# Attention over a running state: Q by the state of four sequences in one block of 32x32 tiles, and attention banks seeded with the result

## The chip, the cores and the metric

One core of one Trainium2 chip. The metric is the time of one execution on the device in microseconds (us); lower is better.

## What is computed

One transformer block on `x` of 4 sequences, 4096 tokens, 512 features, float32, 16 heads of 32 features: LayerNorm, causal linear attention, an output projection, LayerNorm and residual; then LayerNorm, a feed-forward layer with inputs and weights rounded to FP6 values with a scale per block of 32, LayerNorm and residual.

```python
q, k = elu(x @ Wq.T + bq) + 1, elu(x @ Wk.T + bk) + 1      # by heads
v = x @ Wv.T + bv
kv_cum = cumsum(einsum('bhtd,bhte->bhtde', k, v), axis=2)  # the state
numerator = einsum('bhtd,bhtde->bhte', q, kv_cum)
denominator = maximum(einsum('bhtd,bhtd->bht', q, cumsum(k, axis=2)), 1e-6)
out = (numerator / denominator) @ Wo.T + bo
x = x + layernorm(out)
x = x + layernorm(mx(layernorm(x)) @ mx(weight).T + bias)
```

## The kernel before, in words

The loop runs over 32 tiles of 128 tokens; a tile holds all four sequences, b = 0 to 3, 512 rows in all. `turn(i, ...)` is written once for each engine, and every engine carries out its steps in exactly that order; semaphores join them. A turn finishes the feed-forward of tile i-1, does the attention of tile i and begins the LayerNorm and transposes of tile i+1. The turns before and behind the loop leave out the part that does not exist.

Products against weights (k, q, v, o, f) are three products of rounded float32 halves (`product3`, L341): 12 matmuls of 512 columns. k(g) and q(g) write the four score banks, one for each group g of four heads. v, o, f, the transposes and the attention outputs share three PSUM banks, `work[0..2]`; `BANK_ORDER` (L36) lists which stage has which bank in which order, and `take` (L332) waits until the stage that had the bank before has been read (table `freed`, L236).

Attention of a sequence b: `scores(b)` (L426) is K by Q inside the tile, a product for each head, in the four score banks; `mask(b)` on VectorE (L868) applies the causal mask, four operations of 128x512, into A. `attend(b)` (L444) first multiplies Q by the state S, one 128x128 matmul for each group (S is kept block-diagonal, four heads of 32x32 in each group, zeros elsewhere, L453), then adds V by A for each head (L460). `state(b)` (L465) adds K by V of the tile to the state, which PSUM holds all the time; ScalarE copies it to S in four pieces for each sequence (L654). `o_hi` (ScalarE, L644) and `o_lo` (VectorE, L876) split the attention output in two halves, and `o(b)` multiplies it by Wo. Behind that stands a chain for each b: `o_bias` and statistics on VectorE, `rstd` on GpSimd (POOL), `o_norm` on ScalarE (L657), `residual` on POOL (L1049), `r_stats` on VectorE, `rstd`, `r_norm` on ScalarE (L660), `quantise` on VectorE (L893: amax, scale, reciprocal, and the product that writes q8), `dequantise` on POOL, transposes `xd` and f(b) in the next turn. Between them stand, for the next tile, `x_transposes(b)` on TensorE (PE), `x_hi(b)` and `x_norm(b+1)` on ScalarE and `x_lo(b)` on VectorE; x_norm(b+1) overwrites the tile xn that x_transposes(b) reads. Q is divided by the denominators (`denominators`, `invert`, `spread`, `divide`) before it is used.

The order on PE in the second half of a turn: kn(0), spread, f(3), scores(0), v(1), x(0), attend(0), state(0), kn(1), scores(1), v(2), o(0), x(1), attend(1), state(1), kn(2), scores(2), v(3), o(1), x(2), attend(2), state(2), kn(3), scores(3), x(3), o(2), attend(3), state(3); o(3) comes behind k(0) of the next turn. ScalarE's order there:

```python
kn(0); f_norm(2); x_hi(i + 1, 0); x_norm(i + 1, 1); o_hi(0); state(0); kn(1); f_norm(3)
x_hi(i + 1, 1); x_norm(i + 1, 2); o_hi(1); state(1); o_norm(i, 0); kn(2); r_norm(i, 0)
x_hi(i + 1, 2); x_norm(i + 1, 3); o_hi(2); state(2); kn(3); o_norm(i, 1); x_hi(i + 1, 3)
r_norm(i, 1); o_hi(3); state(3)
```

Of the kernel before, what the change touches and what calls it, by code (L numbers as in the profile page):

```python
# [12 lines left out]
P = 128  # L13
# [47 lines left out]
def build(nc, x, wq, wk, wv, wo, wf, bq, bk, bv, bo, bf, consts, out):  # L61
    ctx = ExitStack()
    with ctx:
# [47 lines left out]
        S = sb("S", [P, NSEQ, G, P])  # L111
# [78 lines left out]
        s_set = sem("s_set")  # L190
        xn_set = sem("xn_set")
# [36 lines left out]
        STAGE = {"k": V[:], "q": QT[:], "v": S[:].rearrange("p b g t -> p b (g t)"),  # L228
# [21 lines left out]
        def had_before(stage, here, before):  # L250
# [6 lines left out]
            return None  # L257

# [72 lines left out]
        def _(pe):  # L331
            def take(i, stage, here, before):  # L332

                found = had_before(stage, here, before)
                if found is None:
                    return
                other, turns = found
                reader, per = freed[other[0]]
                pe.wait_ge(reader, count(i + turns + tile_of(other), other[1], per))

# [17 lines left out]
            def transposes(stage, src):  # L358
                for g in range(G):
                    last = nc.tensor.transpose(bank(stage)[:, g * P:(g + 1) * P], src(g), ident[:])  # L360
                return last
# [14 lines left out]
            def turn(i, here, before):  # L376
# [16 lines left out]
                def v(b):  # L393
                    if cur:
                        take(i, ("v", b), here, before)
                        weights(i, "v")
                        by_row("v", b, xT_hi, xT_lo, slice(b * P, (b + 1) * P)).then_inc(v_mm, 1)

                def denominators():
                    if cur:  # L400
                        take(i, ("den", 0), here, before)
# [37 lines left out]
                def kn(b):  # L439
                    if cur:  # L440
                        take(i, ("kn", b), here, before)
                        transposes(("kn", b), lambda g: KT[:, g, b, SEG - P:SEG]).then_inc(kn_tr, 1)

                def attend(b):  # L444
                    if cur:
                        take(i, ("att", b), here, before)
                        if first:
                            pe.wait_ge(state_zeroed, 1)
                        else:
                            pe.wait_ge(s_set, count(i - 1, b))  # L450
# [731 lines left out]
```

## Time and profile before

| | us |
|---|---|
| median of 3 runs | 2689.52 (2688.79 to 2692.34) |
| the profiled execution | 2689.53 |
| its span, first to last instruction | 2687.7 |
| PE busy | 2503.3 (93%) |
| VectorE (DVE) busy | 2171.5 (81%) |
| ScalarE (ACT) busy | 1255.2 (47%) |
| GpSimd (POOL) busy | 1092.2 (41%) |

The share of busy time is an average over the run. What a step is worth is read from the timeline of one turn: an engine starts an instruction when the one before it on the same engine lets it and when what it waits for has been signalled. A timeline row gives the start and the duration; successive instructions of an engine overlap, so the step of an operation is the distance between two starts. The idle time in brackets names who ended it. A float32 matmul leaves two records, one in float32r one.

### The profile page before, as it was taken

The numbers are of one execution on the slowest core, as the hardware profiler recorded it, in microseconds if no ns is written. First come the engines' busy times: TensorE is split into PE (matmuls) and PEld (weight loads), VectorE is DVE, ScalarE is ACT, GpSimd is POOL, SyncE is SP. The second block draws the span as 40 slices with busy tenths as digits, with TensorE's granted clock in tenths as the row PEclk, the third lists the DMA queues.
The fourth block names the chain that finished last, engine by engine and source line by source line (L and its number), as shares of the span: only waits on it lengthen the run. The fifth ranks groups of instructions, "written<-read, shape, count | busy, mean of one in ns | idle before, by whom it ended". The sixth has DMA issues, their size and how long they took to land.

```text
span 2687.7 us, 62620 instructions
## 1 busy us (share of the span) xinstructions
PE 2503.3 (93%) x24082; PEld 2061.4 (77%) x24082; DVE 2171.5 (81%) x4175; ACT 1255.2 (47%) x2314; POOL 1092.2 (41%) x1482
## 2 busy tenths in 40 slices
PE   5999999999999999999999999999999999999996
PEld 4777778777778777778777787777777777877775
DVE  6778888788888788888888887888888888878885
ACT  4444445444454444454444544444544445444442
POOL 1343444334443334443344433444434444333443
PEclk8999999999999999999999999999999999999998
DMA  4011100111011111001111011110111110111000
GB/s 148 21 40 47 41 29 31 39 47 43 30 36 39 39 47 43 27 31 39 47 47 32 30 39 39 47 43 27 36 38 44 47 34 28 39 39 47 31 25 24
DMA packets 57483, 107.55 MB, mean 40 GB/s; under 512 B 6768, under 2 KB 7152, under 8 KB 56816
## 3 DMA queue, kind: packets, MB, share of 16 engines
q1 hardware_dynamic: 57456, 107.18, 12.3%
q8 instruction: 18, 0.29, 0.0%
q14 instruction: 9, 0.07, 0.0%
HBM read 73.60 MB, written 33.55 MB: 40 GB/s over the span
## 4 chain that ended last, share of the span: by engine, by line
PE 43%; DVE 29%; issue 11%; POOL 9%; ACT 6%; DVEq 1%; POOLq 0%; DMA 0%; ACTq 0%; SPq 0%
PE work L343 9%; PE work L345 8%; PE work L344 8%; DVE kc L829 6%; PE score L434 4%; DVE KT L812 4%; PE work L460 4%; PE work L360 4%; PE work L453 3%; DVE A L872 3%; POOL xd L1061 2%; DVE bn_r L789 2%; DVE amax L897 2%; POOL rs_r L1042 2%; DVE QT L812 2%
## 5 line engine op out<-in xcount | busy, mean ns | idle before, releaser
L872 DVE TENSOR_TENSOR A<-score,causal 128x512 f32<-128x512 f32 x512 | 317.5, 683 | 42.3 <-PE score L434 42.2
L597 ACT ACTIVATE o_buf<-x_res,shift_r,rs_r 128x512 f32<-128x512 f32 x128 | 104.7, 818 | 409.2 <-POOL shift_r L1045 409.2
L1052 POOL TENSOR_TENSOR x_res<-x_res,o_buf 128x512 f32<-128x512 f32 x128 | 179.3, 1401 | 210.4 <-ACT o_buf L597 210.4
L593 ACT CAST xT_hi<-work 128x512 fp32r<-128x512 f32 x128 | 74.8, 584 | 384.5 <-PE work L360 384.5
L343 PE MATMUL work<-wv_hi,xT_hi 128*128 128x512 f32 x512 | 216.1, 422 | 0.0
L343 PE MATMUL score<-xT_hi,wk_hi 128*128 128x512 f32 x512 | 206.6, 403 | 6.2 <-issue 6.2
L1042 POOL TENSOR_TENSOR rs_f<-ve_f,minus_half 128x1 f32<-128x1 f32 x128 | 70.3, 549 | 343.9 <-DVE ve_f L793 343.9
L1042 POOL TENSOR_TENSOR rs_r<-ve_r,minus_half 128x1 f32<-128x1 f32 x128 | 96.3, 753 | 278.5 <-DVE ve_r L793 278.5
L343 PE MATMUL score<-xT_hi,wq_hi 128*128 128x512 f32 x512 | 206.5, 403 | 0.0
L343 PE MATMUL work<-wo_hi,oT_hi 128*128 128x512 f32 x512 | 202.7, 396 | 2.9 <-DVE oT_lo L879 2.6
L344 PE MATMUL work<-wv_lo,xT_hi 128*128 128x512 f32 x512 | 202.0, 394 | 0.0
L345 PE MATMUL work<-wv_hi,xT_lo 128*128 128x512 f32 x512 | 201.4, 393 | 0.0
L345 PE MATMUL score<-xT_hi,wk_lo 128*128 128x512 f32 x512 | 200.4, 391 | 0.0
L344 PE MATMUL score<-xT_lo,wq_hi 128*128 128x512 f32 x512 | 200.3, 391 | 0.0
L344 PE MATMUL score<-xT_lo,wk_hi 128*128 128x512 f32 x512 | 200.2, 391 | 0.0
L345 PE MATMUL work<-wo_hi,oT_lo 128*128 128x512 f32 x512 | 200.1, 391 | 0.0
L345 PE MATMUL score<-xT_hi,wq_lo 128*128 128x512 f32 x512 | 199.9, 390 | 0.0
L344 PE MATMUL work<-wo_lo,oT_hi 128*128 128x512 f32 x512 | 199.3, 389 | 0.0
L1042 POOL TENSOR_TENSOR rs_o<-ve_o,minus_half 128x1 f32<-128x1 f32 x128 | 70.4, 550 | 303.9 <-DVE ve_o L793 303.7
L884 DVE TENSOR_TENSOR o_buf<-work,bias_o 128x512 f32<-128x512 f32 x128 | 87.9, 687 | 112.7 <-PE work L345 112.7
L453 PE MATMUL work<-QT,S 128*128 128x128 f32 x1024 | 138.4, 278 | 29.4 <-DVE xT_lo L803 29.4
L621 ACT ACTIVATE exp_t<-exp_t 128x512 f32<-128x512 f32 x256 | 161.1, 629 | 0.0
(130 smaller groups left out, 6957.9 us busy)
## 6 DMA issues: line engine op xcount, KB each, us to landing
x_in<-in_x SPq DMA_DIRECT2D x128, 256.0 KB, 2.8
x_res<-in_x SPq DMA_DIRECT2D x128, 256.0 KB, 2.6
out<-f_buf SPq DMA_DIRECT2D x96, 256.0 KB, 2.0
out<-xd SPq DMA_DIRECT2D x32, 256.0 KB, 2.0
V<-in_wk SPq DMA_DIRECT2D x1, 1024.0 KB, 7.8
QT<-in_wq SPq DMA_DIRECT2D x1, 1024.0 KB, 8.7
kc<-in_wo SPq DMA_DIRECT2D x1, 1024.0 KB, 10.2
A<-in_wf SPq DMA_DIRECT2D x1, 1024.0 KB, 11.9
```

Source lines behind the costliest of these rows:

```text
L343: nc.tensor.matmul(dst, st_hi(c), mv_hi(c), start=(c == 0), stop=False)
L344: nc.tensor.matmul(dst, st_hi(c), mv_lo(c), start=False, stop=False)
L345: last = nc.tensor.matmul(dst, st_lo(c), mv_hi(c), start=False, stop=(c == G - 1))
L360: last = nc.tensor.transpose(bank(stage)[:, g * P:(g + 1) * P], src(g), ident[:])
L434: last = nc.tensor.matmul(score_bank[j][:, g, :], KT[rows, g, b, SEG - P:SEG], QT[rows, g, cols], start=True, stop=True)
L453: nc.tensor.matmul(att[:, g, :], S[:, b, g, :], QT[:, g, b * P:(b + 1) * P], start=(g == 0), stop=False, skip_group_check=True)
L621: nc.scalar.activation(exp_t[:, g % 2, :], exp_t[:, g % 2, :], ACT.Exp, scale=-1.0).then_inc(exp_done, 1)
L812: nc.vector.tensor_tensor(dst, by_seq(exp_t[:, g % 2, :]), dst, ALU.add).then_inc(added, 1)
L829: nc.vector.tensor_tensor_scan(kc[:, g, :, :].rearrange("p b t -> p (b t)"), in_seq[:].rearrange("p b t -> p (b t)"), KT[:, g, :, :].rearr ...
L872: nc.vector.tensor_tensor(A[:, j, :, :], score_bank[j][:], causal[:].unsqueeze(1).to_broadcast([P, G, P]), ALU.mult).then_inc(a_set, 1)
L1042: nc.gpsimd.tensor_tensor(rs[n][:, b:b + 1], ve[n][:, b:b + 1], minus_half[:], ALU.pow).then_inc(rs_set[n], 1)
L1052: nc.gpsimd.tensor_tensor(x_res[:, b, :], x_res[:, b, :], o_buf[:, b % 2, :], ALU.add).then_inc(r_set, 1)
```

## The change

The products of Q with the state leave `attend(b)`. A new step `past_products` on PE, between f(3) and v(1), computes them for all four sequences, a 32x32 tile of the array for each head: rows j (head within the group), columns g (group), 64 matmuls of 128 columns into the four score banks. ScalarE copies the four banks to a new SBUF tile `past_att` (`past`), scores(0) wait for these copies, and before each attend(b) ScalarE copies that sequence's part into the attention bank (`seed`); V by A is added to it. v(1), v(2) and v(3) each stand one stage earlier on PE, mask(0) comes behind v_bias(1) and f_stats(3) on VectorE. S holds only the 32x32 blocks and is copied once a turn. The rows of the attention output change place, with Wo laid out to match on the host. `BANK_ORDER` changes with the order. The transposes set the start flag on the first of four only.

```diff
-    (("v", 1), W1), (("x", 0), W2), (("att", 0), W0), (("kn", 1), W2),
-    (("v", 2), W1), (("o", 0), W2), (("x", 1), W0), (("att", 1), W1), (("kn", 2), W0),
-    (("v", 3), W2), (("o", 1), W0), (("x", 2), W1), (("att", 2), W2), (("kn", 3), W1),
-    (("x", 3), W0), (("o", 2), W1), (("att", 3), W0),
+    (("v", 1), W1), (("v", 2), W2), (("x", 0), W0), (("att", 0), W1), (("kn", 1), W2),
+    (("v", 3), W0), (("o", 0), W1), (("x", 1), W2), (("att", 1), W0), (("kn", 2), W1),
+    (("o", 1), W2), (("x", 2), W0), (("att", 2), W1), (("kn", 3), W2),
+    (("x", 3), W0), (("o", 2), W1), (("att", 3), W2),
-        S = sb("S", [P, NSEQ, G, P])
+        S = sb("S", [P, NSEQ, G, DH])
+        past_att = sb("past_att", [P, NSEQ, HPG, P])
...
                 def scores(b):
                     if cur:
                         if b == 0:
-                            pe.wait_ge(qn_set, count(i, 3))
+                            pe.wait_ge(past_set, count(i, HPG - 1))
...
-                def attend(b):
+                def past_products():
+                    if cur:
+                        if first:
+                            pe.wait_ge(state_zeroed, 1)
+                        else:
+                            pe.wait_ge(s_set, count(i - 1, 0, 1))
+                        wait_apart(pe, qn_set, count(i, 3))
+                        for b in range(NSEQ):
+                            for g in range(G):
+                                for j in range(HPG):
+                                    rows = slice(j * DH, (j + 1) * DH)
+                                    last = nc.tensor.matmul(score_bank[j][g * DH:(g + 1) * DH, b, :], S[rows, b, g, :],
+                                                            QT[rows, g, b * P:(b + 1) * P], start=True, stop=True)
+                        last.then_inc(past_mm, 1)
+
+                def attend(b):
                     if cur:
-                        take(i, ("att", b), here, before)
...
-                        for g in range(G):
-                            nc.tensor.matmul(att[:, g, :], S[:, b, g, :], QT[:, g, b * P:(b + 1) * P],
-                                             start=(g == 0), stop=False, skip_group_check=True)
                         pe.wait_ge(a_set, count(i, b * HPG + HPG - 1, 16))
                         pe.wait_ge(v_set, count(i, b))
-                        for g in range(G):
-                            for j in range(HPG):
+                        pe.wait_ge(seeded, count(i, b))
+                        att = by_group(bank(("att", b))[:])
+                        for j in range(HPG):
+                            for g in range(G):
                                 feats = slice((g * HPG + j) * DH, (g * HPG + j + 1) * DH)
-                                last = nc.tensor.matmul(att[j * DH:(j + 1) * DH, g, :], V[:, b, feats],
+                                last = nc.tensor.matmul(att[g * DH:(g + 1) * DH, j, :], V[:, b, feats],
...
                 f(3)
+                past_products()
+                v(1)
                 scores(0)
-                v(1)
+                v(2)
                 x_transposes(0)
                 attend(0)
                 state(0)
                 kn(1)
                 scores(1)
-                v(2)
+                v(3)
...
                 kn(2)
                 scores(2)
-                v(3)
                 if cur:
                     o(i, 1)
...
+                def past(j):
+                    if cur:
+                        act.wait_ge(past_mm, count(i, 0, 1))
+                        nc.scalar.copy(past_att[:, :, j, :], score_bank[j][:]).then_inc(past_set, 1)
+
+                def seed(b):
+                    if cur:
+                        take(act, i, ("att", b), {0}, set())
+                        if b == 0:
+                            act.wait_ge(past_set, count(i, HPG - 1))
+                        nc.scalar.copy(bank(("att", b))[:],
+                                       past_att[:, b, :, :].rearrange("p j t -> p (j t)")).then_inc(seeded, 1)
+
+                def state():
+                    if cur:
+                        act.wait_ge(st_mm, count(i, NSEQ - 1))
+                        nc.scalar.copy(S[:], state_bank[:]).then_inc(s_set, 1)
...
                 kn(0)
                 f_norm(2)
+                for j in range(HPG):
+                    past(j)
                 if nxt:
                     x_hi(i + 1, 0)
                     x_norm(i + 1, 1)
+                seed(0)
                 o_hi(0)
-                state(0)
                 kn(1)
                 f_norm(3)
+                seed(1)
                 if nxt:
                     x_hi(i + 1, 1)
                     x_norm(i + 1, 2)
                 o_hi(1)
-                state(1)
                 if cur:
                     o_norm(i, 0)
                 kn(2)
+                seed(2)
                 if cur:
                     r_norm(i, 0)
...
                 o_hi(2)
-                state(2)
                 kn(3)
+                seed(3)
                 if cur:
                     o_norm(i, 1)
...
                 f_bias(3)
-                mask(0)
                 v_bias(1)
                 f_stats(3)
+                mask(0)
+                v_bias(2)
                 if nxt:
                     x_lo(i + 1, 0)
                 o_lo(0)
                 mask(1)
-                v_bias(2)
+                v_bias(3)
...
                     r_stats(i, 0)
-                v_bias(3)
-                if cur:
                     o_bias(i, 1)
```

## Rows read from the trace of the kernel before

**Rows 1.** The page: busy shares by engine, and the chain that ended last.

```profile
PE 2503.3 (93%) x24082; PEld 2061.4 (77%) x24082; DVE 2171.5 (81%) x4175; ACT 1255.2 (47%) x2314; POOL 1092.2 (41%) x1482
...
PE 43%; DVE 29%; issue 11%; POOL 9%; ACT 6%; DVEq 1%; POOLq 0%; DMA 0%; ACTq 0%; SPq 0%
```

**Rows 2.** Timeline of PE: start, duration, line, what, [idle before, releaser].

```profile
1210.82 1.08 PE L409 MATMUL work<-kc,den_sel 128*32 128x128 f32 x32 [2.12 <-DVE kc L266]
...
1218.77 1.17 PE L434 MATMUL score<-QT,KT 32*128 32x128 f32 x32
1219.87 0.50 PE L343 MATMUL work<-wv_hi,xT_hi 128*128 128x512 f32 x1
...
1222.73 0.60 PE L360 MATMUL work<-ident,xn 128*128 128x128 f32 x4
1223.16 1.06 PE L453 MATMUL work<-QT,S 128*128 128x128 f32 x8
1224.15 1.08 PE L460 MATMUL work<-A,V 128*32 128x128 f32 x32
1225.04 0.48 PE L475 MATMUL state_bank<-V,Kn 128*32 128x32 f32 x32
1225.45 0.66 PE L360 MATMUL work<-ident,KT 128*128 128x128 f32 x4
...
1240.05 0.39 PE L343 MATMUL work<-wo_hi,oT_hi 128*128 128x512 f32 x1
...
1242.77 0.60 PE L360 MATMUL work<-ident,xn 128*128 128x128 f32 x4
...
1251.63 1.16 PE L453 MATMUL work<-QT,S 128*128 128x128 f32 x8 [0.94 <-DVE xT_lo L803]
...
1278.32 0.47 PE L343 MATMUL work<-wf_hi,xdT_hi 128*128 128x512 f32 x1 [0.98 <-DVE xdT_lo L912]
```

**Rows 3.** Two stretches: length, busy PE, PEld, DVE, ACT, POOL, granted clock, DMA, GB/s.

```profile
1218.77:1254.30 35.53, 34.38 (x517) 29.12 (x517) 26.75 (x54) 14.20 (x30) 9.89 (x16) 1.00 0.19 59
1254.30:1300.49 46.19, 43.09 (x236) 34.75 (x236) 40.52 (x78) 24.66 (x43) 24.26 (x30) 1.00 0.07 23
```

**Rows 4.** Timeline of ACT in the first stretch.

```profile
1223.36 0.59 ACT L593 CAST xT_hi<-work 128x512 fp32r<-128x512 f32 x1 [6.39 <-PE work L360]
1223.84 0.82 ACT L597 ACTIVATE xn<-x_in,shift_x,rs_x 128x512 f32<-128x512 f32 x1
...
1242.02 0.82 ACT L597 ACTIVATE o_buf<-x_res,shift_r,rs_r 128x512 f32<-128x512 f32 x1 [3.74 <-POOL shift_r L1045]
...
1245.34 0.59 ACT L647 CAST oT_hi<-work 128x512 fp32r<-128x512 f32 x1 [0.63 <-PE work L460]
...
1247.39 0.82 ACT L597 ACTIVATE o_buf<-o_buf,shift_o,rs_o 128x512 f32<-128x512 f32 x1
```

**Rows 5.** Timeline of DVE, from mask(2) to the next turn's phi_k(1).

```profile
1237.28 2.48 DVE L872 TENSOR_TENSOR A<-score,causal 128x512 f32<-128x512 f32 x4 [0.69 <-PE score L434]
1239.68 0.68 DVE L789 BATCH_NORM_STATS2 bn_r<-x_res 128x6 f32<-128x512 f32 x1
...
1245.96 0.69 DVE L879 TENSOR_TENSOR oT_lo<-work,oT_hi 128x512 fp32r<-128x512 f32 x1 [0.46 <-ACT oT_hi L647]
...
1247.89 0.69 DVE L905 TENSOR_TENSOR q<-o_buf,rxs 128x512 fp8e4<-128x512 f32 x1
...
1257.08 1.78 DVE L905 TENSOR_TENSOR q<-o_buf,rxs 128x512 fp8e4<-128x512 f32 x1
1258.78 0.68 DVE L789 BATCH_NORM_STATS2 bn_r<-x_res 128x6 f32<-128x512 f32 x1
...
1266.13 0.69 DVE L812 TENSOR_TENSOR KT<-exp_t,KT 128x512 f32<-128x512 f32 x1 [1.10 <-ACT exp_t L621]
```

**Rows 6.** Timeline of POOL: residual(1) and residual(2).

```profile
1248.36 1.37 POOL L1052 TENSOR_TENSOR x_res<-x_res,o_buf 128x512 f32<-128x512 f32 x1 [2.35 <-ACT o_buf L597]
...
1257.01 1.30 POOL L1052 TENSOR_TENSOR x_res<-x_res,o_buf 128x512 f32<-128x512 f32 x1 [1.36 <-ACT o_buf L597]
```

More of the change, by code:

```diff
@@ L257, in had_before, with take @@
             return None
+        def take(engine, i, stage, here, before):
+            found = had_before(stage, here, before)
+            if found is None:
+                return
+            other, turns = found
+            reader, per = freed[other[0]]
+            engine.wait_ge(reader, count(i + turns + tile_of(other), other[1], per))
         def tokens(t, g):
@@ L331, in _ @@
         def _(pe):
[L332 to L339, printed above, removed]
             def product3(dst, st_hi, st_lo, mv_hi, mv_lo):
@@ L359, in transposes @@
                 for g in range(G):
-                    last = nc.tensor.transpose(bank(stage)[:, g * P:(g + 1) * P], src(g), ident[:])
+                    last = nc.tensor.matmul(bank(stage)[:, g * P:(g + 1) * P], src(g), ident[:], is_transpose=True,
+                                            start=(g == 0), stop=(g == G - 1), skip_group_check=True)
                 return last
@@ L394, in v @@
                     if cur:
-                        take(i, ("v", b), here, before)
+                        take(pe, i, ("v", b), here, before)
                         weights(i, "v")
@@ L400, in denominators @@
                     if cur:
-                        take(i, ("den", 0), here, before)
+                        take(pe, i, ("den", 0), here, before)
                         if first:
@@ L467, in state @@
                         pe.wait_ge(kn_set, count(i, b))
-                        if b > 0:
-                            pe.wait_ge(s_set, count(i, b - 1))
-                        elif not first:
-                            pe.wait_ge(s_set, count(i - 1, NSEQ - 1))
+                        if b == 0 and not first:
+                            pe.wait_ge(s_set, count(i - 1, 0, 1))
                         for g in range(G):
@@ L481, in x_transposes @@
                     if nxt:
-                        take(i, ("x", b), here, before)
+                        take(pe, i, ("x", b), here, before)
                         pe.wait_ge(xn_set, count(i + 1, b))
@@ L486, in o @@
                 def o(tile, b):
-                    take(i, ("o", b), here, before)
+                    take(pe, i, ("o", b), here, before)
                     pe.wait_ge(oT_set, count(tile, b))
@@ L493, in xd_transposes @@
                     if prev:
-                        take(i, ("xd", b), here, before)
+                        take(pe, i, ("xd", b), here, before)
                         pe.wait_ge(xd_set, count(i - 1, b))
@@ L499, in f @@
                     if prev:
-                        take(i, ("f", b), here, before)
+                        take(pe, i, ("f", b), here, before)
                         pe.wait_ge(xdT_set, count(i - 1, b))
@@ L641, in kn @@
                         act.wait_ge(kn_tr, count(i, b))
+                        if b > 0:
+                            act.wait_ge(st_mm, count(i, b - 1))
+                        elif not first:
+                            act.wait_ge(st_mm, count(i - 1, NSEQ - 1))
                         nc.scalar.copy(Kn[:], bank(("kn", b))[:]).then_inc(kn_set, 1)
@@ L647, in o_hi @@
                         nc.scalar.copy(oT_hi[:], by_group(bank(("att", b))[:])).then_inc(oT_hi_set, 1)
-                def state(b):
+                def past(j):
                     if cur:
-                        act.wait_ge(st_mm, count(i, b))
-                        for j in range(HPG):
-                            rows = slice(j * DH, (j + 1) * DH)
-                            last = nc.scalar.copy(S[rows, b, :, rows], state_bank[rows, b, :, :])
-                        last.then_inc(s_set, 1)
+                        act.wait_ge(past_mm, count(i, 0, 1))
[11 more added lines that the diff above has]
+                        nc.scalar.copy(S[:], state_bank[:]).then_inc(s_set, 1)
                 def o_norm(tile, b):
@@ L739, in turn @@
                 o_hi(3)
-                state(3)
+                state()
             for b in range(NSEQ):
```

13 lines of the change are left out of this document (8 added, 5 removed).

## The prediction

> **What bounds the kernel now.** I read the page first: the matmul engine (PE) is busy 93% of the span and VectorE (DVE) 81%, and the chain that ended last is PE 43%, DVE 29%, POOL 9%, ACT 6% [rows 1]. So PE sets the end most of the time, but it is not alone. Then the timeline of PE, where I cut a turn of the loop at the start of scores(0) (1218.77, called 0 from here on) and at k(0) of the next turn (1254.30, that is 35.53) [rows 2]. The first piece, 35.53 us, is attention and the o products, the second, 46.19 us, projections and feed-forward; together 81.72 us, and 32 such turns are 2615 of the 2687.7 us. The table by stretches shows PE busy 34.4 of 35.5 us in one and 43.1 of 46.2 us in the other, DVE 26.8 and 40.5 [rows 3]. PE's idle places are three, and behind each stands DVE: 2.12 us before the denominators, 0.98 us before f(1) and 0.94 us before attend(3) [rows 2]. The change lies in the first piece; whether its lateness survives the second one has to be asked of DVE there.
>
> **What goes and what comes on PE.** Removed: four blocks of Q by S, each 0.99 us from its start to that of the next block (1223.16 to 1224.15) [rows 2]: 3.96 us a turn. The stall of 0.94 us in front of the last of them goes as well: its bank will belong to kn(3) before it, no longer to x(3), so it need not wait for x_lo(3). Something else is late there, see below. Added: past_products, 64 matmuls of 32x32 weights by 128 columns. A matmul in float32 leaves two records (16 matmuls, x32), so 128 records. No row has both row and column tiling. Bounds: the state block, 32 records of 32 columns in 0.41 us, is 12.8 ns a record, so 1.6 us for 128; the A block, the same width of weights and 128 columns, four column tiles at once, is 0.90 us for 32, so 3.6 us if only four tiles ever run together [rows 2]. Sixteen tiles leave the array four times the room of the A block (0.9 us), so the rate of issue should decide, which is the state block's: I take 1.9 us with the entry. The Trainium skill, page "TensorE: Matmul & The Clock Gate", section "Back-to-back issue gap", has a floor of about 25 ns from start to start; our state block goes at 12.8 ns, so the trace disagrees, and by that floor the block would be 3.2 us, 1.3 us a turn worse than my value. A reordering costs nothing by itself: v(1) to v(3) each move one stage forward, the loops in attend swap while each output still walks over four column tiles, and the start flags of the transposes change no instruction.
>
> **The seed of sequence 0 stands in the wrong place.** On ACT seed(0) is queued behind x_hi(next,0) and x_norm(next,1). x_hi(0) waits for x_transposes(0), and that is the very last thing that PE does before attend(0). After that block ACT needs 0.20 us to see it, 0.48 to the next start, 0.72 for x_norm (0.82 less the tenth by which ACT's instructions overlap), about 0.6 for the seed and 0.03 for the signal [rows 2, 4]: PE stands 2.03 us, with state(0), kn(1) and scores(1) queued behind. No row copies from SBUF to PSUM; 0.48 us (the step after a copy out of PSUM) and 0.82 us (an activation from SBUF) bound it, and the sum moves by 0.2 us at most. The four copies past(0..3) (about 2.3 us) are hidden under v(1), 2.86 us; without that cover they would hold scores(0). Seeds 1 to 3 come in time. The new timetable on PE, from my row pitches (product 2.86 us, or 2.72 behind another product, scores 1.10, A 0.90 or 1.0 after a stop, state 0.43, kn 0.6, x transposes 0.43): past 0, v(1) 1.9, scores(0) 4.75, v(2) 5.85, x(0) 8.7, attend(0) 11.16, scores(1) 13.15, v(3) 14.25, o(0) ends 19.83, attend(1) 20.27, scores(2) 22.2, o(1) 23.3 to 26.15, x(2) 26.15, attend(2) 26.6. Before, o(1) ended at 24.00 (1242.77); PE is 2.15 us late here although nothing but the seed has stopped it yet.
>
> **What is late next: the chain through r_norm(0).** With v(3) moved forward, o(0) ends later, and between it and o(1) there is a product less to hide its LayerNorm. DVE does mask(2), then r_stats(0). Before, mask(2) ran 18.51 to 20.91 and r_norm(0) started on ACT at 23.25, 2.34 us after r_stats(0) [rows 4, 5]. Now scores(2) end at 23.3, mask(2) runs 23.4 to 25.8, r_stats(0) starts at 25.8, and r_norm(0) at 28.14. Behind it on ACT are x_hi(2), x_norm(3) and o_hi(2), whose inputs are there at 26.8: they run at 28.86, 29.34 and 30.06. So o_lo(2) on DVE comes at 30.7, x_transposes(3) stand 0.6 us and o(2) 0.7 us: o(2) runs 31.4 to 34.25. Then DVE has quantise(0) before mask(3): q8(0) starts 1.93 us after o_lo(2), the mask 0.6 us after that [rows 5], and the mask takes 2.4 us.
>
> **A collision in quantise(0).** q8(0) takes 0.69 us alone, but 1.78 us when it is issued at 1257.08, 0.07 us after POOL began the 1.30 us residual at 1257.01; it ends 0.55 us after POOL [rows 5, 6]. Now count from o_hi(2): q8(0) follows at 0.62+1.93 = 2.55 us. On ACT o_hi(2), kn(3), seed(3) (new, 0.5) and o_norm(1) follow at once, and residual(1) on POOL starts 0.48+0.48+0.50+0.82+0.15 = 2.43 us after it. In the kernel before, without the seed, but with the four copies of S ahead of kn(3), residual(1) began half a microsecond after q8(0): 1248.36 against 1247.89 [rows 5, 6]. Now POOL is ahead by 0.1 us, and q8(0) should end at 34.4 instead of 33.3. mask(3) then runs 34.3 to 36.7; attend(3) starts at 36.84 after 2.6 us of idle PE, and k(0) at 38.55 instead of 35.53: PE is 3.0 us late.
>
> **Does the other piece give it back?** No. x_lo(3), r_stats(1) at 37.3, r_norm(1) at 39.7, o_hi(3) behind it on ACT, o_lo(3) 41.0, q8(1) in collision with residual(2) as today, r_stats(2) at 44.2 against 40.01 (1258.78) before: DVE is 4.2 us late, 1.2 us more than PE. From there on DVE runs without a pause up to xd_lo(1), which f(1) waits for; its one idle place, 1.10 us before phi_k(1), is itself fed by the loop o_bias(3), POOL, o_norm(3), k(1)'s exponential [rows 5], which starts with the same late DVE. So f(1) and the denominators come 4.2 us later than now, and the stall at f(1) takes up the rest. The period becomes 81.7+4.2 = 85.9 us.
>
> **The sum.** Turns 0 to 30: 31 x 4.2 = 130 us. Turn 31 has no next tile, so no x_hi before the seed: 4.2 less the 2.0 us of that stall, about 2 us. The smaller memset of S (under 1.3 us of POOL in turn 0) and one ACT copy of the state instead of four pieces per sequence lie beside PE: nothing. The profiled execution took 2689.53 us, its span 2687.7 and 1.8 around it, which is the median of 2689.52 too. 2689.5+132 = 2822; I say 2820.
>
> **Rivals.** (1) The collision in quantise(0) is missed by its tenth of a microsecond: the mask starts at 33.2, attend(3) at 35.7, r_stats(2) at 43.07, 3.06 us late: 31 x 3.06+1 = 96, 2785 us. For it: my margin is 0.1 us. (2) The tiles do not run sixteen at a time but four, 3.6 us for the block: 1.7 us a turn more, 53 us on top, 2873 us. (3) TensorE's clock. In the steady loop the granted clock is 1.00 of full in both stretches [rows 3], with stalls up to 2.12 us in them. New ones of 2.0 and 2.6 us come. If a stretch of a few microseconds per turn went to the half level, 1.2 GHz, 1.7 us a turn would be added: about 2875 us. (4) The other side: PE's own sum decides, since r_norm(0) is early enough after all and ACT is never blocked. Then a turn changes by -3.96-0.94+1.9+2.03+0.3 (restarts) = -0.7 us, 22 us in all: 2667 us. It decides if r_norm(0) can start by 26.8, when x_hi(2) has its input; it misses that by 1.3 us, since the mask ahead of r_stats(0) on DVE can't start before scores(2) are there. That the change does not do what it says can't hide: its instructions run whatever they compute.
>
> **How the numbers follow.** Forecast 0.55, rival 1 0.25, rivals 2 and 3 together 0.12, rival 4 with its neighbours up to no change 0.08. The range leaves out the ends of 2, 3 and 4, and takes in 1 with a block of 1.6 us and a chain half a microsecond shorter per turn (2785-9-16 = 2760) and the forecast with 1 us a turn more (2850, rounded up): 2758 to 2855. This kernel can tell 0.2%, 5 us. Faster 0.05, same 0.03, slower 0.92.
>
> **What would show it.** The period on PE from denominators to denominators: 85.9 us. past_products 1.9 us long. An idle place of 2.0 us before attend(0), released by ACT's seed; one of 1.5 to 2.6 us before attend(3), released by mask(3); ACT's r_norm(0) waiting for POOL while the PSUM of x(2) is ready; q8(0) long (1.8 us) or short (0.7 us) tells the forecast from rival 1. Wrong it would be if attend(0) starts within half a microsecond of the transposes, or the stalls at f(1) and the denominators shrink by what attention has lost.

## The result, and the profile after

The changed kernel takes 2896.73 us (median, 2896.39 to 2898.53), the kernel before 2689.91 us on the same chip: a ratio of 1.077, with a 95% interval of 1.0757 to 1.0783. That is slower, as forecast, but by 207 us, not by 130, and the time lies above the range. The profiled execution has a span of 2894.8 us and a mean granted clock of 0.958, where before had 0.991.

The page of after: busy shares by engine, the granted clock in 40 slices, the DMA queues, the chain that ended last, and the costliest groups (busy us, mean ns of one | idle before, releaser). It answers to [rows 1].

```profile
PE 2508.8 (87%) x27154; PEld 2026.1 (70%) x27154; DVE 2162.9 (75%) x4175; ACT 1272.8 (44%) x2090; POOL 1089.0 (38%) x1482
...
PEclk8999999999999999999999999999999999999998
...
q8 instruction: 281, 4.60, 0.7%
...
PE 43%; DVE 29%; issue 14%; ACT 7%; POOL 7%; DVEq 0%; POOLq 0%; DMA 0%; SPq 0%; ACTq 0%
...
L348 PE MATMUL score<-xT_hi,wk_hi 128*128 128x512 f32 x512 | 229.0, 447 | 116.9 <-issue 116.9
```

PE's busy time is what it was (2508.8 us, 2503.3 in [rows 1]), though it has 2.1 us less to do in a turn; the rest of the span, PE's idle time, grew from 184.4 to 386.0 us. Three lines have no place in any step of the prediction. The matmul records grew from 24082 to 27154, which is 96 for each of the 32 tiles. The queue of instruction fetches moved 281 packets of 16 KB, the kernel before only 18. And the first product of a turn, k, has 116.9 us of idle time put down to "issue", where the same group before has 6.2 us. The two lines of the kernel before:

```profile
q8 instruction: 18, 0.29, 0.0%
...
L343 PE MATMUL score<-xT_hi,wk_hi 128*128 128x512 f32 x512 | 206.6, 403 | 6.2 <-issue 6.2
```

The timeline of PE, which answers to [rows 2]; a turn goes here from the denominators at 1305.34 to those at 1394.20, and 1313.28 is the 0 of the prediction:

```profile
1305.34 1.08 PE L416 MATMUL work<-kc,den_sel 128*32 128x128 f32 x32 [2.15 <-DVE kc L280]
...
1313.28 1.90 PE L463 MATMUL score<-QT,S 32*32 32x128 f32 x128
1315.12 0.50 PE L348 MATMUL work<-wv_hi,xT_hi 128*128 128x512 f32 x1
...
1324.61 1.08 PE L476 MATMUL work<-A,V 128*32 128x128 f32 x32 [1.97 <-ACT work L679]
...
1343.68 0.65 PE L366 MATMUL work<-ident,xn 128*128 128x128 f32 x4 [0.50 <-DVE xT_lo L836]
...
1344.88 0.47 PE L348 MATMUL work<-wo_hi,oT_hi 128*128 128x512 f32 x1 [0.55 <-DVE oT_lo L912]
...
1349.11 1.08 PE L476 MATMUL work<-A,V 128*32 128x128 f32 x32 [1.23 <-DVE A L905]
...
1354.59 0.79 PE L348 MATMUL score<-xT_hi,wk_hi 128*128 128x512 f32 x1 [4.11 <-issue]
...
1379.98 0.47 PE L348 MATMUL work<-wf_hi,xdT_hi 128*128 128x512 f32 x1 [0.50 <-DVE xdT_lo L945]
...
1394.20 1.08 PE L416 MATMUL work<-kc,den_sel 128*32 128x128 f32 x32 [2.14 <-DVE kc L280]
```

The period is 88.86 us (81.72 before, 85.9 forecast). Read from the top: the block of 32x32 tiles lasts 1.84 us to the next start; the stall before attend(0), released by ACT's seed, 1.97 us; the two small ones before the transposes and o(2) 0.50 and 0.55 us; attend(3) starts at 35.83. Then comes the row that no step of the prediction has: at the loop's back edge (the branch from its last instruction to its first) PE waits 4.11 us for nothing that the timeline names, and the first matmul behind it takes 0.79 us.

The same two pieces as in [rows 3] (length, busy PE, PEld, DVE, ACT, POOL, granted clock, DMA, GB/s):

```profile
1313.28:1354.59 41.31, 32.96 (x613) 26.83 (x613) 28.34 (x58) 17.31 (x29) 11.08 (x18) 0.96 0.18 53
1354.59:1402.03 47.44, 44.80 (x236) 36.13 (x236) 38.53 (x74) 22.12 (x36) 22.98 (x28) 0.96 0.07 23
```

The first piece grew by 5.78 us: 3.9 us at the back edge (4.11 against 0.2), the rest, 1.9 us, is attention. The second grew by 1.25 us although DVE is busy 2 us less in it (38.53 against 40.52). Around the back edge the clock was at its lower level, 1.2 GHz, for a while, as this window shows (0.71 of full on average over 7 us):

```profile
1354.50:1361.50 7.00, 6.91 (x22) 5.60 (x23) 2.92 (x8) 1.85 (x4) 2.09 (x3) 0.71 0.02 5
```

DVE and POOL at the disputed place, which answer to [rows 5, 6]:

```profile
1345.97 0.69 DVE L938 TENSOR_TENSOR q<-o_buf,rxs 128x512 fp8e4<-128x512 f32 x1
...
1356.40 0.68 DVE L822 BATCH_NORM_STATS2 bn_r<-x_res 128x6 f32<-128x512 f32 x1
```
```profile
1346.02 1.79 POOL L1084 TENSOR_TENSOR x_res<-x_res,o_buf 128x512 f32<-128x512 f32 x1 [2.66 <-ACT o_buf L612]
```

The two still meet, but DVE is first by 0.05 us: its instruction takes 0.69 us and POOL's 1.79. That is rival 1's case, and r_stats(2) comes at 43.12 where rival 1 has 43.07.

### The profile page after: what moved, and what is told of

It is laid out like the page before. It is cut to its first block, busy times and chain, and to the rows that moved or that the text cites. A ratio compares the mean times of both kernels' runs of the same rounds, so it can differ in the third digit from the quotient of the medians.

```text
span 2894.8 us, 68478 instructions
## 1 busy us (share of the span) xinstructions
PE 2508.8 (87%) x27154; PEld 2026.1 (70%) x27154; DVE 2162.9 (75%) x4175; ACT 1272.8 (44%) x2090; POOL 1089.0 (38%) x1482
## 4 chain that ended last, share of the span: by engine, by line
PE 43%; DVE 29%; issue 14%; ACT 7%; POOL 7%; DVEq 0%; POOLq 0%; DMA 0%; SPq 0%; ACTq 0%
PE work L348 8%; PE work L350 7%; PE work L349 7%; DVE kc L862 5%; DVE A L905 5%; PE score L441 4%; DVE KT L845 3%; PE work L476 3%; PE work L366 3%; PE score L463 2%; PE score L348 2%; ACT xn L612 2%; PE score L349 2%; PE score L350 2%; DVE QT L845 1%
## 5 line engine op out<-in xcount | busy, mean ns | idle before, releaser
L348 PE MATMUL score<-xT_hi,wk_hi 128*128 128x512 f32 x512 | 229.0, 447 | 116.9 <-issue 116.9
L1084 POOL TENSOR_TENSOR x_res<-x_res,o_buf 128x512 f32<-128x512 f32 x128 | 191.4, 1495 | 178.5 <-ACT o_buf L612 178.5
L845 DVE TENSOR_TENSOR KT<-exp_t,KT 128x512 f32<-128x512 f32 x128 | 122.3, 956 | 142.8 <-ACT exp_t L636 142.8
L476 PE MATMUL work<-A,V 128*32 128x128 f32 x4096 | 139.6, 277 | 101.0 <-ACT work L679 60.9
L349 PE MATMUL score<-xT_lo,wk_hi 128*128 128x512 f32 x512 | 220.4, 430 | 0.0
L350 PE MATMUL score<-xT_hi,wk_lo 128*128 128x512 f32 x512 | 217.6, 425 | 0.0
L348 PEld LDWEIGHTS score<-xT_hi,wk_hi 128*128 128x128 f32 x512 | 110.3, 215 | 144.1 <-issue 120.0
L349 PE MATMUL work<-wo_lo,oT_hi 128*128 128x512 f32 x512 | 200.2, 391 | 0.0
L476 PEld LDWEIGHTS work<-A,V 128*32 128x32 f32 x4096 | 105.8, 110 | 132.6 <-issue 78.3
L878 DVE TENSOR_TENSOR V<-work,bias_v 128x512 f32<-128x512 f32 x128 | 87.9, 687 | 135.3 <-PE work L350 135.3
L1074 POOL TENSOR_TENSOR rs_r<-ve_r,minus_half 128x1 f32<-128x1 f32 x128 | 83.8, 654 | 276.7 <-DVE ve_r L826 276.7
## 6 DMA issues: line engine op xcount, KB each, us to landing
A<-in_wf SPq DMA_DIRECT2D x1, 1024.0 KB, 11.5
```

The lines of the kernel that those rows point to most:

```text
L348: nc.tensor.matmul(dst, st_hi(c), mv_hi(c), start=(c == 0), stop=False)
L349: nc.tensor.matmul(dst, st_hi(c), mv_lo(c), start=False, stop=False)
L350: last = nc.tensor.matmul(dst, st_lo(c), mv_hi(c), start=False, stop=(c == G - 1))
L476: last = nc.tensor.matmul(att[g * DH:(g + 1) * DH, j, :], V[:, b, feats], A[:, j, g, :], start=False, stop=True, skip_group_check=True)
L845: nc.vector.tensor_tensor(dst, by_seq(exp_t[:, g % 2, :]), dst, ALU.add).then_inc(added, 1)
L878: nc.vector.tensor_tensor(V[:, b, :], bank(("v", b))[:], bias_v[:], ALU.add).then_inc(v_set, 1)
```

## The experiments

Every kernel below does the whole work. Times are medians; the ratio is to the kernel before on the same chip. The time at the lower clock, half of full, is worked out as 2 x (1 - mean granted clock) x span: 243 us in after, 48 us in before. Some of it falls on idle time, where it costs nothing.

### The place of PE's loop

The theory: PE's loop has grown by 96 matmuls and 96 weight loads, so that it no longer stays in the instruction memory, and every turn fetches all of it again. The trace has 1,547 records of PE for one turn of the loop before (752 matmuls, 752 weight loads, 43 of control) and 1,732 after. I take 256 instructions to a packet of 16 KB; that is an estimate from the trace of before, which has a packet every 266 records ahead of the loop, where each instruction runs once. The loops are then 6.0 and 6.8 packets' worth, or blocks. The loop runs 30 of the 32 turns and so takes its back edge 29 times. By the times of the packets, before fetches nothing between 182 and 2565 us, while after has nine packets in every turn of the loop: 281 = 20 + 9 x 29. Two of them, 1.2 and 1.7 us long, stand one behind the other from 1350.16 to 1353.06; the wait runs from 1350.48 to k(0) at 1354.59. The rival: the wait is the seed's or DVE's lateness under another name. A loop of 1,732 touches seven blocks when its first instruction stands in one of the places (slots) 0 to 60 of a block of 256, and eight from any other slot.

```diff
-            with pe.Fori(1, TILES - 1) as i:
+            tensor = mybir.EngineType.PE
+            with nc.Fori(1, TILES - 1, engines=OrderedEngineSet([tensor]), head_slot={tensor: 0}) as i:
```

> The changed kernel, with the first instruction of PE's loop laid at the start of a block of 256 instructions (slot 0); nothing else differs. The loop of PE has about 1,730 instructions by my count (848 matmul records, as many weight loads, 36 of control), 6.8 blocks. Theory A, the loop no longer stays in PE's instruction memory: from slot 0 it lies in 7 blocks instead of 8, stays resident like the kernel before, the packets of the instruction queue fall from 281 to about 20, the idle place before k(0) from 4.1 to about 0.25 us, the clock is 1.00 there, and the time is that of rival 1 in the prediction, 2785 us (2765 to 2800). Theory B, the 4.1 us are a wait that the profile doesn't show (on x_lo(3) or the state): nothing changes, 2897 us. Theory C, any loop of this size is fetched again, wherever it starts: 281 packets, 2897 us.

Measured: 2828.56 us, 1.0521 (1.0475 to 1.0567), 68 us less than after. From its page:

```profile
q8 instruction: 20, 0.33, 0.0%
...
L349 PE MATMUL score<-xT_hi,wk_hi 128*128 128x512 f32 x512 | 206.8, 404 | 6.6 <-issue 6.6
```

The fetches and the idle time of k(0) are back at what they were, with nothing else changed. But 110 us of idle time went and only 68 us of the time, which stays above the 2765 to 2800 us expected. Of the rest 32 us came back in front of f(1): from 24.6 us of idle time in after to 56.8 us here. And the price of the lower clock did not go away, it moved behind the other stalls (mean 0.971, some 164 us; PE busy 2516.3 us against 2508.8). Its timeline of PE:

```profile
905.69 0.47 PE L349 MATMUL work<-wf_hi,xdT_hi 128*128 128x512 f32 x1 [1.63 <-DVE xdT_lo L947]
...
919.89 1.62 PE L417 MATMUL work<-kc,den_sel 128*32 128x128 f32 x32 [2.11 <-DVE kc L281]
...
940.73 1.93 PE L477 MATMUL work<-A,V 128*32 128x128 f32 x32 [1.97 <-ACT work L681]
```

Both blocks behind a stall of 2 us are long in this turn: 1.62 and 1.93 us, where the same blocks at full clock take 1.08. It is not so in every turn. By the clock's records the 4 us from the start of attend(0) hold some lower clock in 24 of 32 turns here, and in 2 of 32 in after, where the stall of 1.97 us is the same; the 4 us from the start of the denominators do in 13 of 31 turns here, in 2 in after and in 4 in before.

The second kernel leaves the loop where it is, and asks for a hint at the back edge instead (`hint_back_edge=True` in place of `head_slot`):

> The changed kernel, with a prefetch hint for PE's back edge at the top of each turn; the order and the work are the same. Theory A: the blocks are still fetched every turn (about 280 packets or more), but the first one ahead of the branch, so the idle place falls from 4.1 to under 1 us, the half clock behind it goes, and the time is 2785 to 2800 us. Theory B: 2897 us, unchanged.

Measured: 2825.91 us, 1.0511 (1.0462 to 1.0561), the same as slot 0, but with 20 packets, not some 280. So it says nothing of whether a hint hides a fetch; there was no fetch to hide. Neither expectation had that. The hint is itself an instruction, one more in the turn. Ahead of the loop the two traces record the same 1,641 instructions on PE, so nothing recorded moves the loop's first one; whether it stands elsewhere for another reason, or the hint itself keeps the blocks, is open.

To have the place alone, I gave the kernel before a loop that is longer by 72 instructions that do nothing for the result (four increments of an unread semaphore ahead of each product), 1,619 in all, and put its head once at slot 0 (seven blocks), once at slot 200 (eight). All else is the same in the two.

```diff
             def product3(dst, st_hi, st_lo, mv_hi, mv_lo):
+                for _ in range(4):
+                    pe.sem_inc(padded, 1)
...
-            with pe.Fori(1, TILES - 1) as i:
+            with nc.Fori(1, TILES - 1, engines=OrderedEngineSet([tensor]), head_slot={tensor: 200}) as i:
```

> The kernel before, with 72 to 80 instructions a turn more on PE that only raise a semaphore nobody waits for, four ahead of each product of 12 matmuls, and the loop laid at slot 0: about 1,620 instructions, 6.3 blocks, 7 blocks touched. Theory A: resident, about 20 packets of instructions, and 2690 us plus what the increments cost, 0 to 60 us. Theory C (size alone decides, not the place) can't say where its limit is between 1,547 and 1,732.

> The same instructions as before_pad_slot0, only the loop is laid at slot 200 of a block, so that it touches 8 blocks. Theory A: every block is fetched again each turn, about 280 packets, 3.9 us more idle before k(0) and 1.8 us of k(0) at half clock, less 0.5 us at f(1), where PE waits for DVE today: 4 to 5.5 us a turn, 120 to 165 us slower than before_pad_slot0. Theories B and C: the same time as before_pad_slot0, within 5 us.

Measured: slot 0 2694.83 us, 1.0026 (1.0014 to 1.0037); slot 200 2890.97 us, 1.0753 (1.0722 to 1.0785). From the page of slot 0, then that of slot 200:

```profile
q8 instruction: 19, 0.31, 0.1%
...
L347 PE MATMUL score<-xT_hi,wk_hi 128*128 128x512 f32 x512 | 206.4, 403 | 26.5 <-issue 26.5
```
```profile
q8 instruction: 280, 4.59, 0.7%
...
L347 PE MATMUL score<-xT_hi,wk_hi 128*128 128x512 f32 x512 | 234.2, 457 | 154.4 <-issue 154.4
```

The same instructions cost 196 us more when they stand 200 places further on: 128 us of that is idle time in front of k(0) (4.4 us at each of the 29 back edges), and PE's busy time grew by 69 us (2505.1 to 2574.3), with the time at the lower clock up from 38 to 237 us. Here too the extra packets are nine to a back edge: 280 = 19 + 9 x 29. The mechanism is shown: the place alone decides whether the loop is fetched again. That it costs 196 us here and 68 us in after can be read off the same two sums: in after the right place took 70 us from PE's idle time (386.0 to 315.7) and nothing from its busy time. The expectation was for 120 to 165 us: the wait it had about right, the clock's price too small, and the 0.5 us that it took off at f(1) did not come (35.8 and 36.1 us of idle time there).

### The two placements on ACT

With the loop at slot 0, 140 us over before remain. The prediction's first suspect is seed(0) behind x_hi(next,0) and x_norm(next,1):

```diff
                     past(j)
+                seed(0)
                 if nxt:
...
                     x_norm(i + 1, 1)
-                seed(0)
```

> The changed kernel with PE's loop at slot 0, and ScalarE's seed(0) ahead of x_hi(next,0) and x_norm(next,1). The idle 1.97 us before attend(0) should fall below 0.5 us (it then waits for mask(0)). Theory A1, the wait passes through: attention, the chain through r_norm(0) and the next turn all come 1.9 us earlier, and the half clock behind this stall (in about every second turn of after_slot0) goes too: 31 x 1.9 = 59 us, and up to 50 us of clock: 2720 to 2770 us against 2828 of after_slot0. Theory B1, another chain holds attention just as long (the o and r LayerNorms behind o(0)): under 15 us gained.

Measured: 2736.11 us, 1.0167 (1.0137 to 1.0196), 92 us less. In the table of groups the row of the A blocks tells which part went; slot 0 first, then this kernel:

```profile
L477 PE MATMUL work<-A,V 128*32 128x128 f32 x4096 | 148.9, 289 | 100.8 <-ACT work L681 61.0 <-DVE A L907 39.9
```
```profile
L477 PE MATMUL work<-A,V 128*32 128x128 f32 x4096 | 138.4, 276 | 39.8 <-DVE A L907 39.8
```

61.0 us of idle time released by ACT's seed are gone. The other 31 us go with the clock: the mean rose from 0.971 to 0.985, 164 to 82 us at the lower level, of which half, 41 us, is the most that can be lost. In this kernel the stall had a price of its own and one behind it.

Next r_norm(0), moved behind x_hi(2), x_norm(3) and o_hi(2):

```diff
-                if cur:
-                    r_norm(i, 0)
                 if nxt:
...
                 o_hi(2)
+                if cur:
+                    r_norm(i, 0)
```

> As after_slot0_seed, with ScalarE's r_norm(0) moved behind x_hi(2), x_norm(3) and o_hi(2). The prediction's step says that r_norm(0), waiting for POOL, holds these three by 1.4 us and so costs PE 0.6 us before x_transposes(3) and 0.7 us before o(2). If it is right the two idle places (L838 and L914 as releasers, 0.50 and 0.55 us) vanish and the period falls by 0.7 to 1.3 us more: 20 to 40 us less than after_slot0_seed. If the mask of sequence 3 on DVE holds attend(3) whatever comes before, under 5 us.

Measured: 2688.88 us, 1.0000 (0.9988 to 1.0011), 47 us less, a little over what I gave it. The idle time of PE in front of the transposes, released by xT_lo, falls from 18.0 to 2.1 us, that in front of the o products from 29.5 to 11.5 us: 34 us. The prediction had 0.6 + 0.7 us a turn for the same block, 40 us in 31 turns. The clock gives part of the rest (82 to 70 us at the lower level). With three placements (the loop's, the seed's, r_norm's) the changed kernel is level with the one before, and 68 + 92 + 47 = 207 us is the whole of what the change had cost. The shares depend on the order of undoing.

Is it the forward move of v alone that brings the lateness of r_norm(0)? The kernel before with v(1) to v(3) a stage earlier, mask(0) later on DVE and the banks in after's order, without tiles or seeds:

```diff
                 f(3)
-                scores(0)
                 v(1)
+                scores(0)
+                v(2)
                 x_transposes(0)
...
                 scores(1)
-                v(2)
+                v(3)
```

> The kernel before with one part of the change alone: v(1), v(2), v(3) one stage earlier on PE, mask(0) behind v_bias(1) and f_stats(3) on DVE, and the order of the banks that goes with it; Q by S stays in attend, no seed, no new matmuls, loop at slot 0. Worked out as in the prediction: o(0) ends at 16.8 instead of 13.95 us, r_norm(0) starts at 26.1 and holds x_hi(2) by 1.3 us, attend(3) ends about as before, but o_lo(3) comes 1.5 us later on DVE, so the period grows by 1.0 to 1.6 us: 2720 to 2740 us. If the placement of v costs nothing by itself: 2690 us, within 6.

Measured: 2732.33 us, 1.0153 (1.0123 to 1.0182): 42 us, in the expected span. r_norm(0) waits for POOL with x_hi(2) right behind it, 26.0 us after v(1) began (1239.28), where 26.1 was expected:

```profile
1265.29 0.81 ACT L599 ACTIVATE o_buf<-x_res,shift_r,rs_r 128x512 f32<-128x512 f32 x1 [3.68 <-POOL shift_r L1047]
1266.01 0.57 ACT L595 CAST xT_hi<-work 128x512 fp32r<-128x512 f32 x1
```

So "a reordering costs nothing by itself" was true of PE and false of the kernel, as the prediction's later part had it. The size is partly luck: PE's idle time grew by 16 us only (184.4 to 200.2), its busy time by 25 us, and the expectation had no clock in it. The kernel also lies within 4 us of after_slot0_seed (2736.11), which has the same early v: what was left to mend there is what v's move costs.

### Is there something to win?

PE does 2.1 us less in a turn (3.96 - 1.84), 68 us in all, yet nothing of it shows. First, mask(3) ahead of quantise(0) on DVE and o_hi(3) ahead of r_norm(1) on ACT, on top of the last kernel of after:

```diff
                 o_lo(2)
+                mask(3)
                 if cur:
                     quantise(i, 0)
-                mask(3)
```

> As after_slot0_seed_rnorm, with mask(3) ahead of quantise(0) on DVE and o_hi(3) ahead of r_norm(1) on ScalarE. attend(3) should no longer wait for the mask (1.2 us), and o_lo(3) no longer for r_norm(1). By my timetable k(0) then comes at 32.6 us after the start of past_products against 35.5 in the kernel before, and DVE, without idle time from o_lo(3) on, decides the rest: 2640 to 2700 us. If DVE's total work from o(0) on decides, no gain over after_slot0_seed_rnorm.

Measured: 2688.33 us, 0.9992 (0.9980 to 1.0003), no gain, as the rival expectation had it. The stall before attend(3) went (40.1 us of idle time in front of the A blocks before, 0.2 now), and the one in front of f(1) grew:

```profile
L349 PE MATMUL work<-wf_hi,xdT_hi 128*128 128x512 f32 x256 | 122.6, 479 | 76.7 <-DVE xdT_lo L947 76.7
```

It was 57.1 us one kernel earlier, so half of the 40 us came back there. Of the rest 10 us came back in front of k(0), now released by DVE's x_lo(3) (6.5 to 16.3 us), and 9 in front of the o products (11.5 to 20.6). The denominators gave back 31 us (64.0 to 33.0), but the time at the lower clock rose from 70 to 145 us (mean 0.987 to 0.973), of which up to 37 is lost. So what attention wins goes to waits for DVE and to the clock, the largest part at f(1). The next kernel attacks the stall at f(1): q(2) ahead of f(1) on PE, with its work on ACT and DVE. I made the same moves on the kernel before, so that the pair gives the worth of the change. It is not that of the tiles alone: only the changed kernel has the seeds and v's new places.

```diff
                 q(1)
+                q(2)
                 f(1)
...
-                q(2)
                 q(3)
```

> The changed kernel with PE's loop at slot 0, seed(0) first, r_norm(0) behind o_hi(2), o_hi(3) ahead of r_norm(1), DVE's mask(3) and x_lo(3) ahead of quantise(0), and in the projections PE's q(2) ahead of f(1) and xd_transposes(2), with ScalarE's and DVE's steps in the same order. In after_slot0_order the time won in attention came back as 2.28 us of idle PE before f(1), where DVE's xd_lo(1) is late, and 1.8 us of half clock behind it. If q(2), 2.7 us, fills that place, the period falls by about 2 us, and the clock by up to 1.4 us a turn: 2600 to 2650 us. If DVE's chain sets the period anyway (its next signals, for q(3) and the denominators, come no earlier), the idle time moves there: 2675 to 2690 us.

> The kernel before, with every one of those moves that it can take (r_norm(0) behind o_hi(2), o_hi(3) ahead of r_norm(1), mask(3) and x_lo(3) ahead of quantise(0), q(2) ahead of f(1)), loop at slot 0, but Q by S as it was and v where it was. It tells what the tiles are worth once the order is right. By the matmul blocks alone (3.96 us against 1.84) the tiles save 2.1 us a turn, 68 us: if they do, this one is 60 to 75 us slower than after_f1. If the moves are all that helps, the two are within 15 us of each other.

Measured: 2790.93 us, 1.0378 (1.0360 to 1.0395), and 2791.69 us, 1.0379 (1.0362 to 1.0396). The time missed what either theory gave it; that the pair is level is the rival's side of before_f1. The stall moved to f(2) and grew, from 2.28 us to 6.12, with the clock at the lower level behind it (mean 0.956 and 0.958). Why DVE's work for f(2) comes so late then was not taken apart. The timeline of PE in after_f1:

```profile
1336.32 0.76 PE L349 MATMUL work<-wf_hi,oT_hi 128*128 128x512 f32 x1 [6.12 <-DVE oT_lo L947]
```

The last pair puts f(1) back and advances what the denominators and f wait for: on ACT k(3) and xd_hi(1) ahead of r_norm(3), on DVE phi_k(3) and xd_lo(1) ahead of quantise(3).

```diff
                 f_stats(0)
-                if prev:
-                    quantise(i - 1, 3)
                 phi_k(3)
                 xd_lo(1)
+                if prev:
+                    quantise(i - 1, 3)
```

> The changed kernel with the moves of after_f1 but f(1) in its old place; instead, in the projections, ScalarE's feature map of k(3) and xd_hi(1) come ahead of r_norm(3), which waited for POOL in front of them, and DVE's phi_k(3) and xd_lo(1) ahead of quantise(3). xd_lo(1) then comes about 3 us earlier, and the 2.28 us before f(1) and the half clock behind them should go. If PE's own work then sets the period: 2600 to 2650 us. If DVE's work up to the denominators does (it has the same operations to do by then): the idle time moves there, 2660 to 2690 us.

> The kernel before with every move of after_lead that it can take, Q by S and v as they were. In after_f1 and before_f1 (2791 and 2792 us) the tiles were worth nothing, since both waited for the same DVE work before f(2). If that holds here, the two are within 10 us of each other. If PE's own work counts, the smaller block of the tiles (1.84 against 3.96 us) leaves this kernel up to 68 us behind after_lead.

Measured: 2684.33 us, 0.9989 (0.9979 to 0.9999), and 2685.71 us, 0.9993 (0.9983 to 1.0003). Again the pair is level, and the time is that of the theory in which DVE sets the period. PE's largest idle time is now in front of the denominators in both, released by kc of DVE; after_lead, then before_lead:

```profile
L417 PE MATMUL work<-kc,den_sel 128*32 128x128 f32 x1024 | 50.3, 357 | 81.1 <-DVE kc L281 74.0 <-DVE wf_lo L799 7.2
```
```profile
L410 PE MATMUL work<-kc,den_sel 128*32 128x128 f32 x1024 | 44.8, 329 | 83.7 <-DVE kc L267 73.9 <-DVE wf_lo L766 9.8
```

In both pairs, each with the same moves and the loop at slot 0, the kernel with the change and the one without end within 1.4 us of each other: 2790.9 and 2791.7 us, 2684.3 and 2685.7. The 68 us that the tiles save on PE do not reach the end. In the last pair it can be read where most of them go: after_lead waits 31.0 us in front of the o products and 46.8 in front of f(2), before_lead 13.3 and 33.7, which is 31 us, and after_lead has some 113 us at the lower clock against 70 (mean 0.979 and 0.987), which is up to 21 more. That the tiles would win nothing with v in its old place is not shown; no such kernel was run. After_lead is the fastest, but 0.1% under before is less than this kernel can tell.

## Why the prediction was right and wrong

- **The step that failed** stands in the part on what goes and what comes on PE: "Added: past_products" prices 128 records by the time that they take to run, 1.9 us, and the sum has no term for the length of the loop in which they stand; so it puts the back edge at nothing, without a reason. Measured in its place: a wait of 4.0 us on average at each of 29 back edges (0.2 before) and a first product mostly at the lower clock, k(0) in 4.67 us where it has 2.85 us before; undone by its placement alone, 68 us. It belongs in the sum as a term: so many instructions in the loop before and after, and the queue of fetches as the row to look at.
- **past_products**: 1.9 us forecast, 1.84 measured, from the rate of issue in the state block's row. Rival 2 (four tiles at a time, 3.6 us) falls.
- **seed(0)**: 2.03 us forecast, 1.97 measured. But its undoing in the placed kernel brought 92 us, not 61: there the clock falls behind this stall in most turns. In the forecast's own kernel it does so in 2 of 32 turns only.
- **r_norm(0)**: forecast on ACT at 28.14, it came at 28.26, and the two small stalls were 0.50 and 0.55 us, where I had 0.6 and 0.7. 40 us forecast, 47 measured.
- **The number after the loop is mended** is luck: with the back edge undone the kernel takes 2828.56 us, near the forecast of 2820, but not by its sum. The collision of quantise(0), worth 1.1 us a turn there, did not come, and the lower clock, which the sum puts at nothing, did: rival 1's timetable gives 2785 us, and 116 us more than before are spent at half clock.
- **The collision in quantise(0)** fell the other way, by 0.05 us. The rows on ACT show why: seed(3) started 0.63 us after kn(3), not the 0.48 that I put in (a copy after another out of PSUM), so POOL's residual came 0.15 us later after o_hi(2) than forecast (2.58 us against 2.43). Rival 1 was the right timetable: attend(3) 35.7, measured 35.83; r_stats(2) 43.07, measured 43.12.
- **Rival 3**, the clock, was the right worry with a price that fits one place (1.8 us at k(0), 1.7 by my estimate), but it was set beside the forecast as an alternative; it came on top of rival 1, behind the back edge's wait, which I had not seen.
- **"Does the other piece give it back?"** In part, where I had said no: in after f(1)'s stall is 0.50 us, 0.98 before [rows 2]. The stall at the denominators stayed, 2.14 against 2.12 us.
- **Rival 4** (PE's own sum decides) fell, and the pairs bear on why: even with the placements mended that were tried, PE's saving gives no gain.

The sum by what is now known: attention 1.9 us late and 0.5 us less at f(1), in 31 turns, and 3.9 us of wait and 1.8 us of lower clock in k(0), at 29 back edges: 31 x 1.4 + 29 x 5.7 = 209 us, where 207 were measured. One turn stands here for all.

The ACT rows of after on which the collision's step stands (kn(3), then seed(3)):

```profile
1343.90 0.59 ACT L661 COPY Kn<-work 128x512 f32<-128x512 f32 x1
1344.53 0.59 ACT L679 COPY work<-past_att 128x512 f32<-128x512 f32 x1
```

The Trainium skill, page "Runtime: NRT & Kernel Launch", section "Instruction fetch mechanics", would have raised the question: it gives PE's instruction memory as 2048 instructions, filled in blocks of 256, and says that a taken branch whose target isn't held stalls for a fetch. The traces agree in kind (281 packets of 16 KB, 4.1 us at the back edge), but not, for PE, with its remark that only two such blocks are held (a remark made of 32 KB, the size that it gives for most engines): a loop of 1,619 instructions that touches seven blocks left 19 packets.

## What to carry to other kernels

Before pricing added instructions by what they take to run, count the instructions of the loop on that engine and look at the queue of instruction fetches on the page: if its packets grow with the number of turns, the loop is fetched every turn, and the place of its first instruction can be worth more than the change. Where the order on a helping engine decides (a seed behind two unrelated activations), the stall's price is its length and what the clock takes behind it, and the second part depends on what else stalls in the turn. And a saving on the busiest engine is worth following to the next stalls down the turn: here what was won in attention came back as waits for DVE and as time at the lower clock.

## What was not expected of the hardware, and what stays open

- **A loop near the limit is held whole or not at all.** 19 to 20 packets with seven blocks of 256 touched, 280 or 281 with eight, and nothing between: that is nine fetches at each back edge, not one, and one more than the blocks that the loop touches. A memory of eight blocks that is also filled with the block behind the loop's end would do this; no run separates that from other causes. That the limit is between seven and eight touched blocks rests on the count of recorded instructions and on two placements of one kernel; a third was not run.
- **Who starts first wins on DVE and POOL.** With DVE first by 0.05 us: 0.69 us on DVE and 1.79 on POOL; with POOL first by 0.07 us: 1.78 and 1.30 [rows 5, 6]. So either DVE loses 1.1 us or POOL 0.5, and a tenth of a microsecond decides which. All the traces of this case agree: in the 897 pairs in which this DVE instruction starts first, by up to 0.5 us, it takes 0.69 us, and in the 280 in which POOL is first by 0.06 to 0.6 us it takes 1.32 to 1.78.
- **The clock's fall behind a stall depends on more than the stall's length.** Before attend(0) the same stall of 1.97 us is followed by some lower clock in 2 of 32 turns in after and in 24 of 32 in after_slot0; before the denominators 2.1 us are, in 4 of 31 turns in before and 13 of 31 in after_slot0. What decides it is open.
- Open too: why the kernel with the hint had 20 packets; and whether DVE's sequence in the second piece can be shortened, which might let the tiles show.
